# Edge layer of a graph network: the sum of gathered and spread rows moves from VectorE to TensorE's accumulation

## The reference, cut to what matters

```python
h = maximum(layernorm(x), 0)
e = concatenate([h[dst], h[src] - h[dst]], axis=-1)      # one row per edge
m = relu(e @ W1 + b1) @ W2 + b2                           # one message per edge
x = x + where(isfinite(out := segment_max(m, dst)), out, 0)
```

## Time and profile before

| | |
|---|---|
| median of three runs | 18585.29 us |
| span of the profiled execution (first to last instruction) | 13809.8 us |
| TensorE, busy share of the span | 51% |
| weight loads of TensorE | 37% |
| VectorE | 66% |
| ScalarE | 43% |
| GpSimd | 57% |
| first and last addition of L1424 | at 563.3 and 5235.4 us |

### The profile page before, as it was taken

One profiled execution on the slowest core, in us unless ns is written; L12 is line 12 of the kernel. 1 busy time (PEld: TensorE's weight loads), 2 busy tenths in 40 slices (PEclk: granted clock), 3 DMA queues, 4 the chain that ended last, 5 costly groups with the idle time before them and its releaser, 6 DMA issues. The chain is left out here.

```text
span 13809.8 us, 283975 instructions
## 1 busy us (share of the span) xinstructions
PE 7082.0 (51%) x96792; PEld 5084.7 (37%) x96792; DVE 9045.7 (66%) x17848; ACT 5948.2 (43%) x10705; POOL 7815.4 (57%) x7194
## 2 busy tenths in 40 slices
PE   2266666666666663998899999700000000000066
PEld 1155555555555552554455555400000000000055
DVE  5388888888888886444444344466666666666585
ACT  0144444444444443776777677522222222222201
POOL 5677777777777773111111111367777777777700
PEclk9866666666666666999899899755555555555598
DMA  7333333333333333886688588422222222222197
GB/s 308 144 112 113 112 114 114 119 112 112 113 112 115 115 114 94 261 265 220 200 263 267 172 265 263 160 72 66 63 66 66 66 63 66 63 63 66 60 361 241
DMA packets 1274431, 1981.83 MB, mean 144 GB/s; under 512 B 256937, under 2 KB 987918, under 8 KB 1268737
## 3 DMA queue, kind: packets, MB, share of 16 engines
q1 hardware_dynamic: 867553, 1059.78, 24.4%
q10 hardware_dynamic: 174288, 612.09, 12.0%
q0 software_dynamic: 231664, 297.80, 8.1%
HBM read 1167.21 MB, written 815.55 MB: 144 GB/s over the span
## 5 line engine op out<-in xcount | busy, mean ns | idle before, releaser
L632 POOL DMA_INDIRECT RF<-tab_edge_b,idx x3125 | 3541.2, 1133 | 1030.6 <-issue 948.6
L1180 POOL DMA_INDIRECT records<-RF,idx x3125 | 3130.6, 1002 | 984.5 <-issue 984.5
L1737 ACT ACTIVATE X<-bk 128x392 uint8<-128x392 f32 x4000 | 1782.6, 495 | 1565.0 <-PE bk L1898 1548.0
L685 DVE TENSOR_TENSOR HM<-iota_b,eqw 128x2048 bf16<-128x2048 bf16 x2000 | 2201.7, 1101 | 342.7 <-PE bk L1898 197.6
L1898 PE MATMUL bk<-HM 128*64 128x98 bf16 x32000 | 1583.2, 247 | 1306.7 <-ACT X L1737 672.8
L1898 PE MATMUL kp<-HM,ident_b 128*64 128x98 bf16 x6250 | 281.7, 283 | 3805.4 <-DVEq L1646 3805.4
L876 POOL DMA_INDIRECT agg<-RF,lastT x372 | 536.9, 1443 | 2856.9 <-ACT RF L808 2766.0
L769 PE MATMUL tp<-HM,RF 128*64 128x512 bf16 x12276 | 2001.2, 379 | 7.9 <-ACT HM L728 2.0
L1898 PEld LDWEIGHTS bk<-HM 128*64 128x64 bf16 x32000 | 1239.8, 134 | 1653.2 <-issue 1571.3
L1898 PEld LDWEIGHTS kp<-HM,ident_b 128*64 128x64 bf16 x6250 | 261.7, 168 | 3826.3 <-issue 3826.3
L775 PE MATMUL om<-HM,RF 128*64 128x512 bf16 x6138 | 1442.3, 379 | 0.0
(11 more groups left out here) (362 smaller groups left out, 14805.4 us busy)
## 6 DMA issues: line engine op xcount, KB each, us to landing
dst_f<-counts SPq DMA_DIRECT2D x465, 512.0 KB, 4.6
RF<-first_rows SPq DMA_DIRECT2D x250, 800.0 KB
counts<-X ACTq DMA_DIRECT2D x250, 784.0 KB
records<-RF ACTq DMA_DIRECT2D x88, 1960.0 KB, 8.2
RF<-records SPq DMA_DIRECT2D x220, 784.0 KB
crow<-counts SPq DMA_DIRECT2D x279, 512.0 KB, 4.7
first_rows<-RF ACTq DMA_DIRECT2D x25, 4000.0 KB, 49.5
edge_rows<-RF ACTq DMA_DIRECT2D x125, 800.0 KB, 8.0
```

The lines of the kernel that those rows point to most:

```text
L632: e.indirect_dma_start(out=ring[:, r, j, :], out_offset=None, in_=table[:, :], in_offset=bass.IndirectOffsetOnAxis(ap=idx[:, r, j:j + 1], ...
L685: return e.tensor_tensor(to[:, 0:n, :].rearrange("p k (q h) -> p k q h", h=2), iota_b[:, 0:m].rearrange("p (q h) -> p q h", h=2).unsqueeze ...
L1180: e.indirect_dma_start(out=records[:, :], out_offset=bass.IndirectOffsetOnAxis(ap=idx2[:, r, j:j + 1], axis=0), in_=msgs[MSG_OF[r]][:, j, ...
L1737: e.activation(staged[u].rearrange("p (r k) -> p r k", k=P)[:, :, k:k + 4], bk[s % 2][:, 0:4 * TILES].rearrange("p (k r) -> p r k", k=4), ...
```

## The change

In `open_slot` VectorE's addition is left out; the semaphore `summed0` is raised right behind the keys' subtraction. In `turn` each transpose becomes two products with the identity matrix, one of `ring` and one of `fill`, the second accumulating on the first in the same place of the bank, so that the sum stands in `tp` as before. Nothing else changes: no wait, no buffer, no order.

```diff
@@ open_slot
                 e.tensor_scalar(ckey[:, :], crow[:, r, 0:CH], node128T[:, bass.ds(b, 1)], None, ALU.subtract)\
                     .then_inc(sem("keyed"), 1)
-                loop_chain(e.tensor_tensor(ring[:, r, :, :], ring[:, r, :, :], fill[:, r, :, :], ALU.add))
                 loop_chain.clear()
                 e.sem_inc(sem("summed0"), 1)
@@ turn
                     m = len(c) * D
-                    last = e.transpose(tp[q % 2][0:m, k * P:(k + 1) * P],
-                                       ring[:, r, c[0]:c[-1] + 1, :], ident[:, :])
+                    to = tp[q % 2][0:m, k * P:(k + 1) * P]
+                    e.matmul(to, ring[:, r, c[0]:c[-1] + 1, :], ident[:, :], start=True, stop=False)
+                    last = e.matmul(to, fill[:, r, c[0]:c[-1] + 1, :], ident[:, :], start=False, stop=True)
                 last.then_inc(sem("turned0"), 1)
```

## The result

The kernel after takes 18849.58 us, the median of four runs (18844.32 to 18869.97); the kernel before took 18601.25 us beside it (18583.72 to 18618.24). The ratio is 1.0137 with a 95% interval from 1.0124 to 1.0149: the change costs 248 us where 130 us of gain were forecast, and 18849.58 lies outside the range of 18400 to 18640.

What follows compares the result with a forecast made beforehand. VectorE, with whatever TensorE makes it wait for, was taken to set the pace at 37.7 us a block. 100 blocks x 1.3 + 25 x 0 = 130 us less: span 13680 plus 4775 gives 18455 us, range 18400 to 18640.

Steps and rivals of the forecast that it cites:

- the 4775 us: Time by which the timed median stands above the traced span; taken as outside the pass and added unchanged to 13680 us.
- Size: Edge pass: 1.3 us gained in each of 100 normal blocks, 0 in 25 behind a jump (every fifth block): 130 us less.
- Clock: TensorE, working without a gap from T+2.3 (T: end of keys' subtraction), reaches full clock between T+5.1 and T+8.1.
- Turn of quarter 1: Between histogram and products of quarter 0, with nothing to hide it: costs its full 1.3 to 2.5 us more.
- VectorE's own chain: Start of quarter 0 in block B, T+12.35 without idleness before it: taken as set by VectorE's own instructions.
- Rival 1: GpSimd becomes the bound: it can give 171 us, so the time stops at 18414 us; chance 0.12.
- GpSimd's lead at the end well below 62 us: Sign of being right: the last key gather's lead over the subtraction reading it, 62.1 us before, shrinks well below that.
- Rival 3: Clock rises where it does now; turns of quarters 0 and 1 at half clock: 135 us more, 18720 us; chance 0.18.
- Rival 4: In TensorE's turns a float32 product costs four turns, not two: 370 us more, 18955 us; chance 0.03.

Runs made afterwards that it cites:

- e5: Kernel before, unchanged, traced on a chip of the long way (kernel before takes about 18.5 ms there, 13.8 in the short way): 18581.37 us.
- e6: Kernel after, unchanged, on a chip of the long way: 18838.36 us, ratio 1.0133 to the kernel before.
- e11: Kernel before with VectorE's addition left out and transposes kept (spread rows missing from the sums), long way: 18557.51 us, ratio 1.0045.
- e17: Kernel after, unchanged, on a chip of the short way: 13719.45 us, ratio 0.9917 to the kernel before.
- e14: Kernel before, unchanged, traced on a chip of the short way: 13808.35 us.
- e15: Kernel before with VectorE's addition left out and transposes kept, short way: 13649.08 us, ratio 0.9871.
- e9: Kernel after with each row gather made for 64 of 128 partitions, long way: 18827.51 us, ratio 1.019 to the kernel before.
- e13: Kernel after with 12 row gathers a block in place of 25, short way: 13670.81 us, ratio 0.9889 to the kernel before.
- e18: Kernel after with 12 row gathers a block in place of 25, another short-way chip: 13687.12 us, ratio 0.9891 to the kernel before.
- e7: Kernel after with the turn of quarter 1 and products of quarter 0 ahead of the histogram, long way: 18879.18 us, ratio 1.015 to the kernel before.
- e2: Kernel before with VectorE's addition left out and transposes kept, first run in the short way: 13668.52 us, ratio 0.9878.

## Why the prediction was wrong

**The step that failed is the last one of the sum:** "since nothing outside the pass is touched I carry over unchanged the 4775 us by which the median stands above the span". A trace 26% shorter than the time it stands for is not a trace of that execution with something around it. It is a trace of another one. Three quarters of the 4775 us were in the very blocks that the change edits, as TensorE's crawl, and there the same edit has the opposite sign. The prediction's last paragraph named it ("if it is made of the same work, the gain may differ there"), but gave it no rival, no price and no chance, and the range didn't reach it.

What the change does in the long way, from e5 and e6, for one block: the histogram ends 0.8 us later, the turn of quarter 1 takes 3.0 in place of 0.9 us (2.1 more), and the products of quarter 0 lead to VectorE's start 0.9 us sooner, because the clock has risen by then. The sum is +2.0 us at quarter 0, the period grows by 2.2, and the pass by 260 us over 124 blocks. The addition's 2.0 us bring nothing (e11). The 0.8 us follow from a count: of the histogram's products 49 come ahead of the crawl before and 36 after, and when the crawl ends, at T+39.4 in both, 8 are left before and 28 after (means over the blocks); 20 more at 0.04 us are 0.8 us. The product instructions added to the turn of quarter 0 take the place of histogram instructions.

By the prediction's own steps, held against the short way, for which its rows stood:

- *Size.* Forecast 100 blocks x 1.3 + 25 x 0 = 130 us less; measured 119 (e17), and within the pass 4671.9 - 4554.2 = 117.7 us between the first and the last subtraction of e14 and e17. That the sum is so near is in part luck, since two terms were off in opposite directions: a block that isn't behind a jump gained 0.9 us (36.4 to 35.5), not 1.3, which is 40 us less over the pass, and one behind a jump gained 1.0 (43.2 to 42.2), not 0, which is 25 us more.
- *Clock.* It rises at T+5.0 (median), where it rose at T+10.2; forecast T+5.1 to T+8.1. The rows of one block of e17 (T = 2106.99) show what that does; compare the histogram and turn of the earlier trace rows:

```profile
2109.91 0.63 PE L1929 MATMUL tp<-ident,RF 128*128 128x128 f32 x2
2110.33 0.63 PE L1930 MATMUL tp<-ident,RF 128*128 128x128 f32 x2
...
2112.21 0.39 PE L1930 MATMUL tp<-ident,RF 128*128 128x128 f32 x2
2112.53 0.23 PE L1897 MATMUL mixed<-HM 128*64 128x98 bf16 x2
...
2114.85 0.49 PE L1929 MATMUL tp<-ident,RF 128*128 128x128 f32 x2
...
2116.51 0.49 PE L1930 MATMUL tp<-ident,RF 128*128 128x128 f32 x2 [0.28 <-issue]
...
2117.29 1.06 PE L1952 MATMUL om<-w_diag,hT 128*128 128x128 f32 x8
```

  The turn of quarter 0 ends at T+5.6 and the histogram, at the full clock, takes 2112.53 to 2114.85 = 2.3 us for 4.2.
- *Turn of quarter 1.* Right: it takes 1.9 us (median over the blocks), 1.8 in the forecast; in the block shown it is 2.44 with an issue pause in it. The histogram ends at T+8.1 (7.9 by the sum), the products start at T+10.2 (9.7) and VectorE follows 1.4 us later (1.3): small amounts, all in one direction, put quarter 0 at T+11.6 and not T+11.0.
- *VectorE's own chain.* In block B I took the start of quarter 0 as set by VectorE's own instructions. It is set by VectorE's wait for the histogram's first half, 3.3 us earlier (the table), which the earlier trace rows had listed (`mixed`, 105 times, 92.9 us) and the sum passed over; the early clock shortens that too.
- *GpSimd.* Rival 1 didn't happen, and "GpSimd's lead at the end well below 62 us" was wrong. The last key gather and the last subtraction of e17:

```profile
L640 POOL DMA_INDIRECT crow<-kr,cix x125: 942/948/1875, 546.8 to 5053.2; - x125
L1422 DVE TENSOR_SCALAR ckey<-crow,node128T x125: 272/300/310, 562.9 to 5117.1; 128x128 f32<-128x128 f32 x125
```

  The lead is 63.9 us, since GpSimd follows VectorE's pace as before, and its own work in a block fell too (28.5 us in one block of e14, 27.5 in one of e17). With the addition out and no products (e15) the rival is real: the lead is gone and VectorE waits for gathers, which caps e15's gain. The same view of e15's subtraction and of its wait:

```profile
L1422 DVE TENSOR_SCALAR ckey<-crow,node128T x125: 278/301/523, 562.6 to 5073.0; 128x128 f32<-128x128 f32 x125
DVE ckey L1422 <- DMA crow<-kr,cix: 106.8, 39, 6.7
```

- *Rival 3* named the right place for the long way and about half of the price (the turn of quarter 1 at half clock before the products of quarter 0: 135 us more forecast, 248 measured), but its condition, a clock that rises no earlier, was not what happened. The clock rises at T+5.0 in the long way as well, and falls back in the crawl, so the turn of quarter 1 stands at half clock by another road.
- *Rival 4* (four turns for a float32 product) is out: 52 records a block in `tp`, 0.11 us apart at the full clock and 0.21 at half, as forecast from the earlier trace rows.

What is shown and what is not: that the crawl, and no time outside the pass, holds the loss is shown by e5 and e6. That the addition is worth nothing in the long way is shown by e11. That the crawl comes with GpSimd's gathers is shown by the stretches alone: in e5, e6 and the trace of the kernel after it is there in every block with gathers and absent in the four without (the second and the last three). In the trace of the kernel after it ends 36.8 us behind the block's first gather and 4.6 us behind its last, with a standard deviation over the same 88 blocks of under 0.1 us. Whether fewer gathers would shorten it was not tested, since e9's edit left GpSimd's time nearly as it was and e13 and e18 met chips of the short way. In the long way no run has the products with the addition kept, so the split of the loss there rests on the traces of e5, e6 and e11. Why two chips crawl and two don't is open.

## What to carry to other kernels

Before anything else hold the span of the trace against the timed runs. If they differ by more than the runs do among themselves, the trace shows another execution, and its rows price a change only for that one: give the time that no row shows a rival of its own, placed in the very stretch that the change edits. Work moved to an engine costs what it costs at the place that the next wait depends on, and the two ways of running here (TensorE dense and fast, or mostly idle and at half clock) gave one edit -119 and, by chip, +246 to +339 us.

## What the runs showed of the hardware

- TensorE can stand still again and again while GpSimd issues indirect DMAs: pauses of 0.5 to 2.6 us in the block shown, with no cause that the profile shows, 31 products in 33 us, in the same program that on other chips has none. It looks like a lack of instructions; no row shows their supply. About the same amount gets through before the crawl: 185 to 190 records of TensorE, weight loads and its queue's included, from T on, in eight of the nine traces of the long way (means over the blocks that don't stand behind a jump), and 198 in e7. Instructions added ahead of it push others into it or behind it.
- It is not TensorE alone. In the last stage of the long way, again beside GpSimd's gathers, ScalarE and VectorE pause too; the waits of e5 from 12700 to 18200 us have these two rows, and those of e14 (9000 to 13500 us) have neither:

```profile
ACT bk L1833 <- issue: 662.7, 198, 8.8
DVE om L1628 <- issue: 118.6, 124, 2.0
```

- The size and the speed of the instruction fetches don't explain it. The rows of the DMA queue for instructions, first short (e14), then long (e5), and in both a packet of 16 KB takes 1.0 us (median):

```profile
q8 instruction: 558, 9.14, 0.3%
```

```profile
q8 instruction: 549, 8.99, 0.2%
```

- An indirect DMA costs GpSimd nearly the same for 64 partitions as for 128 (906 and 948 ns), so fewer gathers save time there and smaller ones don't.
- Less work on VectorE can make a kernel slower: e11, +0.45% (0.28% to 0.61%), against -1.2% and -1.3% for the same edit in the short way (e2, e15).
